# A new order of one batch's work on ScalarE, VectorE and TensorE in the attention part of an attention and mixture-of-experts kernel

## The chip, the cores and the metric

One core of one Trainium2 chip runs the whole program. The metric is the time of one execution on the device in microseconds (us); lower is better.

## What is computed

The input x holds 16 batches of 1024 rows with 256 columns. Two residual blocks follow each other, each closed by a layer norm over the columns.

```python
q = softmax(x @ Wq, axis=-1)              # over the 256 columns
k = softmax(x @ Wk, axis=-2)              # over the 1024 rows of a batch
v = x @ Wv
ctx = einsum('bnd,bne->bde', k, v) * scale
x = layernorm(x + (q @ ctx / 256) @ Wo + bo)
logits = x @ wr.T                          # 8 experts, the best two per row
# each expert takes its first 5120 rows; slot = number of the row among them
y = gelu(x[rows of e] @ w1[e] + b1[e]) @ w2[e] + b2[e]
x = layernorm(x + sum over the row's experts of gate * y)
```

## The kernel before

**Stages.** The first stage is the attention with the routing (Python block `block_a`), batch by batch. The second runs the experts (`block_b`), the third the last layer norm (`block_c`). The change touches the first alone.

**Precision.** A product in full precision is made of three products of a high and a low part (`product`, lines 681 to 687): a tensor x is split into `hi` (a rounded copy that ScalarE makes) and `lo = x - hi` (that VectorE makes). `xt_raw` is x transposed, as loaded; its parts `xt_hi`, `xt_lo` lie in the buffers that the trace calls `w_hi` and `w_lo`.

**One body per batch.** Each engine has a hand-written list of steps for batch b, called `body` (ScalarE from line 377, VectorE from 574, TensorE from 733). Engines run their lists in order and meet only by semaphores. In body b TensorE works on three batches:

- For batch b: `transpose_k(0..3)` puts the exponentials of k into the PSUM tile `t_ps`, ScalarE copies them out (`kt_out`, to `kt`), and `context(0..3)` multiplies them with `x_raw` into `g_ps` (the trace's line 761). ScalarE and VectorE split that sum into `g_hi` and `g_lo`; `maps` multiplies them with Wv·Wo into `m_ps`; VectorE scales that to `m_raw`, which is split in turn (`m_hi`, `m_lo`). `transpose_q`, `qt` on both engines and `attend(0..3)` give the output (line 685 with o_ps and g_ps), and VectorE's `residual(0..3)` adds x.
- For batch b+1: `q_next(0..3)` and `k_next(0..3)` are the logits of q and k. VectorE takes their maxima (`q_maximum` line 483, `k_maximum` line 479), ScalarE the exponentials (`q_softmax` line 355, `k_softmax` line 349). `q_next(j)` needs the PSUM tile that `q_softmax(j-1)` has read; `k_next(2)` needs the first `k_softmax`, `transpose_k(0)` of the following body the second.
- For batch b-1: VectorE computes the layer norm's `statistics`, and in `router` the two best experts (`choose`), the scores' gap times the norm's factor (`scale_gap`, line 533, which waits for GpSimd's `norm_chain`), and from TensorE's `rank` (a prefix sum over rows) the slots (`place`), the addresses (`address`) and the gates (`gates`). ScalarE takes the exponential of the gap (`gate_exp`) and applies the norm (`normalize`, two halves of four instructions). GpSimd then issues 16 scattering DMAs (`scatter`, line 320), and only after them comes its `norm_chain` for the next batch.
- For batch b+2: ScalarE makes `xt_hi` (`split_xt_hi`, line 345) and VectorE `xt_lo` (`split_xt_lo`, line 467). SyncE loads the next `xt_raw` when that is done, between the load of x and the two stores of the normalized batch.

Bodies are numbered 0 to 15. Body 0 has no work for a batch b-1, the last two have no split of x transposed, and the last one has no logits.

Of the kernel before, what the change touches and what calls it, by code (L numbers as in the profile page):

```python
# [6 lines left out]
def build(nc, x, x_t, wq, wk, wv_t, wo, wo_t, bo, bo_t, wr_t, w1, b1_t, w2, b2, out):  # L7
# [38 lines left out]
    with outer:  # L46
# [38 lines left out]
        with ExitStack() as phase:  # L85
# [254 lines left out]
            def _(act):  # L340
# [41 lines left out]
                def body(pair, u, first, last):  # L382
# [19 lines left out]

                    if more:
                        q_softmax(b + 1, 1 - u, 0, None if first else TILES * b)
                    kt_out(0)
                    kt_out(1)
                    kt_out(2)
                    if more:
                        q_softmax(b + 1, 1 - u, 1)
                    kt_out(3)  # L410
                    if split_next:
                        split_xt_hi(b + 2, u)
                    if not first:
                        gate_exp(b - 1)
                        normalize(b - 1, 1 - u, 0)
# [3 lines left out]
                    nc.scalar.activation(g_hi[:, :, :], g_sum, ACT.Copy).then_inc(g_hi_done, 1)  # L419
                    if more:  # L420
                        q_softmax(b + 1, 1 - u, 2)
# [6 lines left out]
                    if more:  # L428
                        k_softmax(b + 1, 1 - u, 0)
                        q_softmax(b + 1, 1 - u, 3)  # L430
                    if not first:
                        normalize(b - 1, 1 - u, 1)
                    qt(2)
                    qt(3)
# [13 lines left out]
            def _(dve):  # L448
# [57 lines left out]
                def router(b, u, state):  # L506
# [28 lines left out]
                    def place():  # L535
                        dve.wait_ge(rank_ready, b + 1)
                        step(V.tensor_tensor(slot[:, :, :], rank_ps, over_tiles(slot_next[:, :]), ALU.add))
                        V.tensor_tensor(slot_next[:, :], slot_next[:, :], total_ps, ALU.add)
                        step(V.tensor_tensor(late[:, :, :], slot[:, :, :], over_tiles(slot_end[:, :]), ALU.is_ge))
                        step(V.scalar_tensor_tensor(slot[:, :, :], late[:, :, :], DROPPED, slot[:, :, :], ALU.mult, ALU.add))  # L540
# [22 lines left out]
                    return choose, scale_gap, place, address, gates  # L563
# [9 lines left out]
                def body(pair, u, first, last):  # L573
# [5 lines left out]
                    if not first:  # L579
                        choose, scale_gap, place, address, gates = router(b - 1, 1 - u, {"k": 0})  # L580
# [3 lines left out]
                    if not first:  # L584
                        dve.wait_ge(r_done, TILES * b)
                        statistics(b - 1, 1 - u)
                        choose()
                    if more:
                        q_maximum(b + 1, 1 - u, 1)
                    dve.wait_ge(k_exp_done, DK * (b + 1))  # L590
# [7 lines left out]
                    if split_next:  # L598
                        split_xt_lo(b + 2, u)
# [5 lines left out]
                    dve.wait_ge(g_hi_done, b + 1)  # L605
                    V.tensor_tensor(g_lo[:, :, :], g_sum, g_hi[:, :, :].bitcast(F), ALU.subtract).then_inc(g_lo_done, 1)
# [31 lines left out]
                    residual(0)  # L638
                    qt(2)
                    residual(1)  # L640
                    qt(3)
                    if more:
                        k_maximum(b + 1, 1 - u, 1)
                    residual(2)
# [5 lines left out]
                choose, scale_gap, place, address, gates = router(NB - 1, 1, {"k": 0})  # L650
                choose()
                scale_gap()
                place()
# [28 lines left out]
            def _(pe):  # L682
# [51 lines left out]
                def body(pair, u, first, last):  # L734
# [17 lines left out]
                    def context(j):  # L752
                        if j == 0:
                            pe.wait_ge(x_loaded[u], 16 * (pair + 1))
                            if not first:
# [38 lines left out]
                    def maps():  # L794
                        pe.wait_ge(g_lo_done, b + 1)
                        if first:
                            pe.wait_ge(wvo_split, 2)
# [22 lines left out]
                    context(2)  # L820
                    if not first:
                        rank(b - 1)
                    context(3)
# [432 lines left out]
```

## Time and profile before

| | us |
|---|---|
| median of 3 runs (2379.13 to 2380.41) | 2379.3 |
| the profiled execution | 2381.19 |
| its span in the trace | 2379.4 |

The profiled execution's span is split by TensorE's work: the attention stage lasts to some 655 us, the experts to 2263 us, the last norm to the end. The view of stretches gives the busy time of each engine in a stretch and the granted clock of TensorE as a share of 2.4 GHz. The timelines list instructions by their start and duration in us; the brackets give how long the engine was idle before the instruction and who released it. A matmul's duration overlaps that of the next one, so distances are read from start to start.

### The profile page before, as it was taken

The page shows a single profiled execution, that of the slowest core. Times are in us where ns is not written, and L with a number is a line of the kernel's source. Part 1 is how long each engine was busy: PE and PEld are TensorE (multiplying, and loading weights), DVE is VectorE, ACT ScalarE, POOL GpSimd, SP SyncE. Part 2 cuts the span into 40 slices and gives each one's busy share as a digit, 9 for nine tenths or more (in the row PEclk, how much of TensorE's full clock was granted, in tenths as well). Part 3 has the DMA queues.
Part 4 walks back from the last instruction along what each step waited for, and adds up shares of the span by engine and source line. Part 5 has one row for each costly group of instructions (what it writes and reads, how often), then busy time and mean ns, then how long its engine had stood idle before and what let it go on. Part 6 is the DMA issues. An engine that isn't in the chain of part 4 may idle for free. (4 is left out here: it accounts for less than half of the span.)

```text
span 2379.4 us, 39592 instructions
## 1 busy us (share of the span) xinstructions
PE 2107.2 (89%) x13648; PEld 1903.9 (80%) x13649; DVE 1133.1 (48%) x2509; ACT 1125.1 (47%) x2009; POOL 1084.2 (46%) x1185
## 2 busy tenths in 40 slices
PE   6988888888279999999999999999999999999910
PEld 5877887787268899988989998888999888889910
DVE  3666666666443344344344334433533533333345
ACT  3454454444234444444444444444444444444437
POOL 0344645545644444444445444444444444444434
PEclk9999999999689999999999999999999999999955
DMA  5233424422234223223224232422322232323268
GB/s 190 89 124 108 124 92 127 129 77 90 71 106 86 40 49 78 46 44 80 44 44 80 44 49 41 84 42 47 78 46 44 44 44 44 44 44 48 43 204 376
DMA packets 134436, 195.29 MB, mean 82 GB/s; under 512 B 19712, under 2 KB 114816, under 8 KB 130176
## 3 DMA queue, kind: packets, MB, share of 16 engines
q0 software_dynamic: 61376, 73.19, 19.2%
q1 hardware_dynamic: 73024, 121.69, 14.9%
q8 instruction: 15, 0.25, 0.0%
q14 instruction: 21, 0.17, 0.0%
HBM read 106.67 MB, written 88.15 MB: 82 GB/s over the span
## 5 line engine op out<-in xcount | busy, mean ns | idle before, releaser
L1035 DVE TENSOR_TENSOR h_lo<-h_ps,h_hi 128x512 fp32r<-128x512 f32 x544 | 376.1, 691 | 762.8 <-ACT h_hi L1002 762.7
L997 ACT ACTIVATE h_ps<-h_ps,b_sb 128x512 f32<-128x512 f32 x544 | 360.1, 662 | 735.3 <-PE h_ps L1103 725.1
L960 POOL DMA_INDIRECT sum_rows<-y,put_idx x276 | 435.8, 1579 | 554.2 <-DVE y L1023 491.2
L1116 PE MATMUL y_ps<-w_hi,h_hi 128*128 128x256 f32 x2176 | 608.7, 280 | 12.8 <-DVE h_lo L1035 12.8
L1116 PE MATMUL y_ps<-w_hi,h_lo 128*128 128x256 f32 x2176 | 605.9, 278 | 0.0
L1116 PE MATMUL y_ps<-w_lo,h_hi 128*128 128x256 f32 x2176 | 604.9, 278 | 0.0
L1103 PE MATMUL h_ps<-bt_hi,w_hi 128*128 128x512 f32 x1088 | 434.3, 399 | 5.9 <-issue 3.5
L1116 PEld LDWEIGHTS y_ps<-w_hi,h_hi 128*128 128x128 f32 x2176 | 408.9, 188 | 36.6 <-DVE h_lo L1035 19.7
L1103 PE MATMUL h_ps<-bt_hi,w_lo 128*128 128x512 f32 x1088 | 430.3, 396 | 0.0
L1103 PE MATMUL h_ps<-bt_lo,w_hi 128*128 128x512 f32 x1088 | 429.5, 395 | 0.0
L1116 PEld LDWEIGHTS y_ps<-w_hi,h_lo 128*128 128x128 f32 x2176 | 409.2, 188 | 17.5
L1116 PEld LDWEIGHTS y_ps<-w_lo,h_hi 128*128 128x128 f32 x2176 | 409.1, 188 | 0.0
L320 POOL DMA_INDIRECT slot_table<-entry,where x256 | 254.4, 994 | 274.2 <-DVE entry L560 197.4
L1002 ACT ACTIVATE h_hi<-h_ps 128x512 fp32r<-128x512 f32 x544 | 326.0, 599 | 17.1
L949 POOL DMA_INDIRECT rows<-x_rows,pick_idx x280 | 274.2, 979 | 125.8 <-issue 64.6
L1103 PEld LDWEIGHTS h_ps<-bt_hi,w_lo 128*128 128x128 f32 x1088 | 204.9, 188 | 45.6
L1103 PEld LDWEIGHTS h_ps<-bt_hi,w_hi 128*128 128x128 f32 x1088 | 205.0, 188 | 38.0 <-issue 4.9
L1103 PEld LDWEIGHTS h_ps<-bt_lo,w_hi 128*128 128x128 f32 x1088 | 205.3, 189 | 30.5
L1051 DVE TENSOR_TENSOR y_raw<-y_ps,b_sb 128x1024 f32<-128x1024 f32 x68 | 83.2, 1224 | 144.8 <-PE y_ps L1116 144.8
L761 PE MATMUL g_ps<-kt,x_raw 128*128 128x256 f32 x512 | 123.4, 384 | 24.0 <-ACT kt L393 24.0
L355 ACT ACTIVATE q_exp<-q_ps,nq_max 128x256 f32<-128x256 f32 x128 | 59.5, 470 | 140.5 <-DVE nq_max L483 137.4
L761 PEld LDWEIGHTS g_ps<-kt,x_raw 128*128 128x128 f32 x512 | 92.4, 190 | 37.5 <-issue 17.0
(190 smaller groups left out, 2697.5 us busy)
## 6 DMA issues: line engine op xcount, KB each, us to landing
xt_raw<-in_x_t SPq DMA_DIRECT2D x16, 1024.0 KB, 4.9
x_raw<-in_x SPq DMA_DIRECT2D x16, 1024.0 KB, 7.0
w_raw<-in_w SPq DMA_DIRECT2D x16, 1024.0 KB, 7.4
x_rows<-x_sb SPq DMA_DIRECT2D x16, 1024.0 KB
sum_rows<-x_sb SPq DMA_DIRECT2D x16, 1024.0 KB
s_in<-sum_rows SPq DMA_DIRECT2D x16, 1024.0 KB, 8.8
out<-s_out SPq DMA_DIRECT2D x16, 1024.0 KB, 6.7
rows<-x_rows,pick_idx POOLq DMA_INDIRECT x280, 2.8
```

The lines of the kernel that those rows point to most:

```text
L320: pool.indirect_dma_start(out=table_dram, out_offset=bass.IndirectOffsetOnAxis(ap=where[u][:, c, t:t + 1], axis=0), in_=entry[u][:, c, t, ...
L355: nc.scalar.activation(q_exp[u][:, t, :], q_ps[:, t % 2, 0:D], ACT.Exp, bias=nq_max[:, u, t:t + 1], accum_out=zq[:, u, t:t + 1]).then_inc( ...
L761: ins = nc.tensor.matmul(g_sum[:, k, :], x_raw[u][:, t, k * P:(k + 1) * P], kt[:, j % 2, i * D:(i + 1) * D], start=(t == 0 and k == 0), st ...
L949: pool.indirect_dma_start(out=rows[u][:, t, :], out_offset=None, in_=x1_dram, in_offset=bass.IndirectOffsetOnAxis(ap=pick_idx[u][:, t:t + ...
L960: pool.indirect_dma_start(out=acc_dram, out_offset=bass.IndirectOffsetOnAxis(ap=put_idx[:, t:t + 1], axis=0), in_=y[:, t, :], in_offset=No ...
L997: nc.scalar.activation(h_ps[:, c, :], h_ps[:, c, :], ACT.Gelu_apprx_tanh, bias=b1_sb[:, bass.ds(e * FT + f, 1)]).then_inc(gelu_done, 1)
L1002: nc.scalar.activation(h_hi[:, c, :], h_ps[:, c, :], ACT.Copy).then_inc(h_hi_done, 1)
L1035: V.tensor_tensor(h_lo[:, c, :], h_ps[:, c, :], h_hi[:, c, :].bitcast(F), ALU.subtract).then_inc(h_lo_done, 1)
L1051: V.tensor_tensor(y_raw[:, :, :], y_ps[:, :, :], b2_sb[:, bass.ds(e * D, D)].rearrange("p (a d) -> p a d", a=1).broadcast_to([P, BT, D]), ...
L1103: ins = nc.tensor.matmul(h_ps[:, f % 4, :], w[:, c:c + P], v[:, k, :], start=(i == 0), stop=(i == 3 * DK - 1))
L1116: ins = nc.tensor.matmul(y_ps[:, t, :], v[:, f % 4, t * P:(t + 1) * P], w[:, c:c + D], start=(f == 0 and t % 2 == 0 and part == 0), stop=( ...
```

## The change

The same instructions run in another order.

- ScalarE: `kt_out(0)` and `kt_out(1)` come ahead of `q_softmax(0)`; `split_xt_hi` ahead of `kt_out(3)`; `q_softmax(1)` behind it. `normalize(0)` moves behind the copy to `g_hi`, `normalize(1)` behind `qt(2)` and `qt(3)`.
- VectorE: `q_maximum(1)` comes ahead of `choose`. The two steps of `place` that read the ranks from PSUM become `ranked`, directly behind `scale_gap`; then comes `g_lo`, and only then `place`, `address` and `q_maximum(2)`. `split_xt_lo` moves from behind `scale_gap` to behind `residual(0)`, late in the body. `residual(2)` comes ahead of the second `k_maximum`.
- TensorE: `rank` comes behind `context(3)`, and in body 0 the wait for the split of Wv·Wo stands at `context(0)` where it stood at `maps`.

```diff
+                    kt_out(0)
+                    kt_out(1)
                     if more:
                         q_softmax(b + 1, 1 - u, 0, None if first else TILES * b)
-                    kt_out(0)
-                    kt_out(1)
                     kt_out(2)
+                    if split_next:
+                        split_xt_hi(b + 2, u)
+                    kt_out(3)
                     if more:
                         q_softmax(b + 1, 1 - u, 1)
-                    kt_out(3)
-                    if split_next:
-                        split_xt_hi(b + 2, u)
                     if not first:
                         gate_exp(b - 1)
-                        normalize(b - 1, 1 - u, 0)
...
                     nc.scalar.activation(g_hi[:, :, :], g_sum, ACT.Copy).then_inc(g_hi_done, 1)
+                    if not first:
+                        normalize(b - 1, 1 - u, 0)
...
-                    if not first:
-                        normalize(b - 1, 1 - u, 1)
                     qt(2)
                     qt(3)
+                    if not first:
+                        normalize(b - 1, 1 - u, 1)
...
                         statistics(b - 1, 1 - u)
-                        choose()
                     if more:
                         q_maximum(b + 1, 1 - u, 1)
+                    if not first:
+                        choose()
...
                         scale_gap()
-                    if split_next:
-                        split_xt_lo(b + 2, u)
+                        ranked()
+                    dve.wait_ge(g_hi_done, b + 1)
+                    V.tensor_tensor(g_lo[:, :, :], g_sum, g_hi[:, :, :].bitcast(F), ALU.subtract).then_inc(g_lo_done, 1)
                     if not first:
                         place()
                         address(prev, scattered)
                     if more:
                         q_maximum(b + 1, 1 - u, 2)
-                    dve.wait_ge(g_hi_done, b + 1)
-                    V.tensor_tensor(g_lo[:, :, :], g_sum, g_hi[:, :, :].bitcast(F), ALU.subtract).then_inc(g_lo_done, 1)
...
                     residual(0)
+                    if split_next:
+                        split_xt_lo(b + 2, u)
                     qt(2)
                     residual(1)
                     qt(3)
+                    residual(2)
                     if more:
                         k_maximum(b + 1, 1 - u, 1)
-                    residual(2)
                     residual(3)
...
                     context(2)
+                    context(3)
                     if not first:
                         rank(b - 1)
-                    context(3)
```

## Rows read from the trace of the kernel before

**Rows 1.** The page, part 1: busy us, share of the span, instructions by engine.
```profile
PE 2107.2 (89%) x13648; PEld 1903.9 (80%) x13649; DVE 1133.1 (48%) x2509; ACT 1125.1 (47%) x2009; POOL 1084.2 (46%) x1185
```

**Rows 2.** Stretches: start:end, length, busy by engine, TensorE clock, DMA share, GB/s.
```profile
243.50:280.60 37.10, 32.84 (x219) 29.67 (x217) 24.38 (x72) 19.54 (x48) 18.55 (x21) 1.00 0.37 114
...
280.60:317.70 37.10, 32.78 (x208) 29.59 (x207) 24.49 (x72) 18.00 (x46) 18.23 (x22) 0.95 0.37 114
```

**Rows 3.** Timeline (start us, duration us): bodies' first q logits, first maximum.
```profile
38.42 0.48 PE L685 MATMUL q_ps<-wq_hi,w_hi 128*128 128x264 f32 x1
...
72.40 0.69 DVE L483 TENSOR_REDUCE nq_max<-q_ps 128x2 f32<-128x512 f32 x1 [0.98 <-PE q_ps L687]
...
252.66 0.69 DVE L483 TENSOR_REDUCE nq_max<-q_ps 128x2 f32<-128x512 f32 x1 [0.98 <-PE q_ps L687]
...
286.50 0.28 PE L685 MATMUL q_ps<-wq_hi,w_hi 128*128 128x264 f32 x1
...
288.18 0.69 DVE L483 TENSOR_REDUCE nq_max<-q_ps 128x2 f32<-128x512 f32 x1 [0.98 <-PE q_ps L687]
...
325.23 0.69 DVE L483 TENSOR_REDUCE nq_max<-q_ps 128x2 f32<-128x512 f32 x1 [0.97 <-PE q_ps L687]
...
546.25 0.69 DVE L483 TENSOR_REDUCE nq_max<-q_ps 128x2 f32<-128x512 f32 x1 [0.98 <-PE q_ps L687]
```

**Rows 4.** Timeline of TensorE around its three waits, in two neighbouring bodies.
```profile
268.02 0.39 PE L704 MATMUL k_ps<-w_hi,wk_lo 128*128 128x512 f32 x1
...
270.33 0.39 PE L685 MATMUL g_ps<-wvo_hi,g_hi 128*128 128x264 f32 x1 [1.91 <-DVE g_lo L606]
...
283.89 0.28 PE L687 MATMUL g_ps<-m_hi,qt_lo 128*128 128x264 f32 x1
...
284.94 0.39 PE L685 MATMUL o_ps<-m_hi,qt_hi 128*128 128x264 f32 x1 [0.76 <-DVE x_sb L629]
...
287.98 1.03 PE L749 MATMUL t_ps<-ident,k_exp 128*128 128x128 f32 x8
...
290.63 1.75 PE L761 MATMUL g_ps<-kt,x_raw 128*128 128x256 f32 x7 [1.62 <-ACT kt L393]
```

**Rows 5.** Timeline of TensorE at the start of the last body.
```profile
578.20 1.03 PE L749 MATMUL t_ps<-ident,k_exp 128*128 128x128 f32 x8
...
579.57 1.97 PE L761 MATMUL g_ps<-kt,x_raw 128*128 128x256 f32 x8 [0.34 <-ACT kt L393]
```

**Rows 6.** Timeline, ScalarE and VectorE in two bodies: what precedes g_lo.
```profile
300.00 2.08 ACT L365 ACTIVATE x_sb<-x_sb,nshift,rstd 128x256 f32<-128x256 f32 x4
...
300.06 2.29 DVE L467 TENSOR_TENSOR w_lo<-xt_raw,w_hi 128x2048 fp32r<-128x2048 f32 x1 [2.29 <-ACT w_hi L345]
...
305.12 0.68 DVE L606 TENSOR_TENSOR g_lo<-g_ps,g_hi 128x512 fp32r<-128x512 f32 x1
...
592.05 0.69 DVE L606 TENSOR_TENSOR g_lo<-g_ps,g_hi 128x512 fp32r<-128x512 f32 x1 [0.57 <-ACT g_hi L419]
```

**Rows 7.** Timeline of VectorE: the scaled gap (L533), the last gate (L560).
```profile
297.60 0.17 DVE L533 TENSOR_TENSOR gap<-gap,rstd 128x8 f32<-128x8 f32 x1 [0.62 <-POOL nshift L314]
...
565.04 0.17 DVE L560 TENSOR_TENSOR entry<-gap_exp,entry 128x8 f32<-128x8 f32 x1
...
589.17 0.17 DVE L533 TENSOR_TENSOR gap<-gap,rstd 128x8 f32<-128x8 f32 x1 [2.71 <-POOL nshift L314]
...
597.09 0.17 DVE L560 TENSOR_TENSOR entry<-gap_exp,entry 128x8 f32<-128x8 f32 x1
```

**Rows 8.** Timeline: a scatter DMA beside a split, and a pause.
```profile
351.11 0.98 POOL L320 DMA_INDIRECT slot_table<-entry,where  x1 [2.14 <-issue]
...
625.91 4.42 DVE L658 TENSOR_TENSOR w_lo<-w_raw,w_hi 128x4096 fp32r<-128x4096 f32 x1
...
626.86 4.43 POOL L320 DMA_INDIRECT slot_table<-entry,where  x1 [3.82 <-DVE entry L560]
```

**Rows 9.** View by tile of xt_raw, its loads' way to memory on the chip.
```profile
DMA to landing us min/median/max: 4.8/4.9/6.0
```

More of the change, by code:

```diff
@@ L430, in body @@
                         q_softmax(b + 1, 1 - u, 3)
+                    qt(2)
+                    qt(3)
                     if not first:
                         normalize(b - 1, 1 - u, 1)
-                    qt(2)
-                    qt(3)
                     if more:
@@ L533, in scale_gap, with ranked @@
                         V.tensor_tensor(gap[:, :], gap[:, :], rstd[:, :], ALU.mult).then_inc(gap_ready, 1)
-                    def place():
+                    def ranked():
                         dve.wait_ge(rank_ready, b + 1)
@@ L538, in place @@
                         V.tensor_tensor(slot_next[:, :], slot_next[:, :], total_ps, ALU.add)
+                    def place():
                         step(V.tensor_tensor(late[:, :, :], slot[:, :, :], over_tiles(slot_end[:, :]), ALU.is_ge))
@@ L561, in gates @@
                         assert state["k"] == ROUTE_STEPS, state["k"]
-                    return choose, scale_gap, place, address, gates
+                    return choose, scale_gap, ranked, place, address, gates
                 def statistics(b, u):
@@ L579, in body @@
                     if not first:
-                        choose, scale_gap, place, address, gates = router(b - 1, 1 - u, {"k": 0})
+                        choose, scale_gap, ranked, place, address, gates = router(b - 1, 1 - u, {"k": 0})
                     if more:
@@ L649, in _ @@
                 statistics(NB - 1, 1)
-                choose, scale_gap, place, address, gates = router(NB - 1, 1, {"k": 0})
+                choose, scale_gap, ranked, place, address, gates = router(NB - 1, 1, {"k": 0})
                 choose()
                 scale_gap()
+                ranked()
                 place()
@@ L754, in context @@
                             pe.wait_ge(x_loaded[u], 16 * (pair + 1))
-                            if not first:
+                            if first:
+                                pe.wait_ge(wvo_split, 2)
+                            else:
                                 pe.wait_ge(r_done, TILES * b)
@@ L795, in maps @@
                         pe.wait_ge(g_lo_done, b + 1)
-                        if first:
-                            pe.wait_ge(wvo_split, 2)
                         for o in range(DK):
```

## The prediction

> **What bounds the kernel now.** Part 1 of the page shows TensorE busy for 89% of the span and no other engine over 48% [rows 1], so I look for time in which TensorE stands still or runs slowly. The view of stretches, laid over one batch, gives 32.8 us of TensorE work in a 37.1 us body, with VectorE at 24.5, ScalarE at 18.0 and GpSimd at 18.2 us; in one neighbour the granted clock was 1.00 over the body and in the other 0.95, that is, part of it at 1.2 instead of 2.4 GHz [rows 2]. The first maximum of the q logits marks the same point of every body: from 252.66 to 288.18 are 35.52 us (no slow time), from 288.18 to 325.23 are 37.05 us [rows 3]. So one fall of the clock costs 1.53 us. The loop's other bodies repeat one of the two lengths; 8 of the 15 bodies ahead of the last have the fall. In each it comes right at `maps`, behind TensorE's wait for `g_lo`.
>
> The timeline of TensorE then shows three waits in a body [rows 4]. (a) From the first k transposes to `context(0)` pass 287.98 to 290.63 = 2.65 us; it waits for `kt`, which ScalarE copies only behind `q_softmax(0)`, which waits for VectorE's maximum. (b) From the last matmul of `k_next(0)` to `maps` pass 268.02 to 270.33 = 2.31 us, where matmuls of this kind follow each other at 0.24 us; it waits for `g_lo`. (c) In front of `attend(3)` pass 283.89 to 284.94 = 1.05 us, where 0.12 us is the pace; it waits for `residual(2)`, queued behind a `k_maximum`.
>
> **The change part by part.** Durations are those of the profiled execution, whose span is 2379.4 us inside 2381.19 us; the median is 2379.3 us. I subtract the saving from the median, as it does not depend on the 1.9 us between the two.
>
> (a) `kt_out(0)` and `(1)` ahead of `q_softmax(0)`. The last body has no `q_softmax`, so it already shows this order: 578.20 to 579.57 = 1.37 us from transposes to `context(0)` [rows 5]. Saving 2.65 - 1.37 = 1.28 us. `q_softmax(0)` gets later by two copies, some 1.1 us, and frees the tile that `q_next(1)` needs; `context(0)`, about 1.8 us long, and two transposes stand ahead of `q_next(1)` and cover that. Without them it would cost up to 1.1 us.
>
> (b) `g_lo` earlier. Now it starts at 305.12, behind the four `normalize` on ScalarE (2.08 us, ahead of `g_hi`), `split_xt_lo` (2.29 us), `place`, `address` and `q_maximum(2)` on VectorE [rows 6]. All of these move behind `g_hi` and `g_lo`. The new order needs `context(3)` for `g_hi`, the ranks for `ranked`, and the scaled gap for both. Let N be the time of the scaled gap after the body's first q logit. From N, `gate_exp`, `g_hi` and `g_lo` remain: in the last body `g_lo` began 592.05 - 589.17 = 2.9 us after the gap [rows 6, 7], of which 2.0 us were the four `normalize` that move away; 0.75 us later `maps` began. So `maps` can start at N + 1.7. TensorE gets there at 268.02 + 0.24 - 250.98 - 1.28 = 16.0 us (250.98 is 252.66 minus the 1.68 us between first logit and maximum, 286.50 to 288.18 [rows 3]). The wait is gone if N is under 14.3. That saves 2.31 - 0.24 = 2.07 us per body, and with it the 1.53 us of slow clock in 8 bodies, as no idle time as long as 1.9 us would be left. `rank` behind `context(3)` only swaps two pieces of TensorE work of 1.1 and 1.6 us.
>
> N comes from GpSimd. It issues 16 scatter DMAs after the last gate and only then the norm chain: from 565.04 + 0.17 to the next scaled gap at 589.17 pass 24.0 us [rows 7]. At 297.60 the gap waited for it too: N is 297.60 - 286.50 = 11.1 us now. In the new body the last gate falls S = 19.4 us after the start (565.21 - 544.57 = 20.6 in body 14, less 1.28 of (a)). So N = 19.4 + 24.0 - P, with P the new length of a body: 12.0 us for P = 31.4.
>
> (b') `split_xt_lo` late. It is moved past `g_lo`, and lands in VectorE's idle time ahead of `qt(2)`, some 2.8 us in the trace; ScalarE delivers `qt_hi(2)` sooner as `normalize(1)` no longer precedes it, so both arrive about together. TensorE has `k_next(2)`, `attend(1)` and `k_next(3)`, some 4.8 us, before it wants `qt_lo(2)`. No cost there; it would be up to 2.3 us if that cover went. But it now runs beside the scatter DMAs, which it never did. A row shows what that does: beside VectorE's split at 625.91 (4.42 us, until 630.33) the DMA issued at 626.86 took 4.43 us instead of 0.98 [rows 8]; it ended 0.96 us after the split. So GpSimd stood still until VectorE was through. A split of 2.29 us then costs GpSimd between nothing (if the two don't meet as they did there) and 2.3 us; I take 2.1 us, the row being of the same instruction on the same kind of operands. N becomes 14.0 us, just under the 14.3. VectorE then reaches the scaling of `m_raw` at N + 4.1 = 18.1 us instead of 17.9, and the split of `m_hi` and the later k exponential follow: 0.2 us per body.
>
> The Trainium skill ("SBUF — State Buffer", Who interferes with whom) says that a VectorE instruction with two SBUF inputs contends with a GpSimd instruction that reads SBUF, and infers that generating DMA descriptors is not held up by such a `tensor_tensor`. By that inference this term would be nought and the result 2.6 us lower; the row above speaks against it, and I go by the row.
>
> SyncE's queue: the load of `xt_raw` waits for `split_xt_lo` and is now issued some 26 us into the body instead of 16, still ahead of the two stores (`normalize(1)` ends about 3 us later) and of the load of x. It is wanted by `split_xt_hi` 10.8 us after the issue, and lands after 4.8 to 6.0 us [rows 9].
>
> (c) `residual(2)` ahead of `k_maximum`: 1.05 - 0.12 = 0.93 us saved. The second k exponential comes 0.9 us later and is wanted by the next body's transposes, behind `q_next(0)`: by my count it ends 0.1 us after TensorE is ready. So 0.1 us is given back.
>
> **The sum.** A loop body without slow clock: 35.52 - 1.28 - 2.07 - 0.93 + 0.1 + 0.2 = 31.5 us; added up piece by piece from the starts on TensorE it is 31.6, which I take. Body 0 has no router: from 38.42 to 72.40 - 1.68 it took 32.30 us, and (a), (c) and 0.1 us at `maps` leave 30.1 us. Bodies 0 to 13 took 546.25 - 1.68 - 38.42 = 506.15 us; they will take 30.1 + 13 x 31.6 = 440.9. Saved: 65.2 us. In body 14 the last gate comes 20.6 - 19.4 = 1.2 us earlier. The attention stage ends by GpSimd: last gate, 24.0 us, last body's `g_lo` and gate, 24 us more, one more scatter. In the last body gap to last gate are 8.1 us (589.17 to 597.26) [rows 7]; without the four `normalize` in front of `g_hi` 6.2. Saved: 1.9 us. GpSimd sometimes pauses 2.1 us in a scatter (the row at 351.11, seen in 2 of 16) [rows 8]. With N so close to its limit nothing hides that any more: 2 us lost. Sum: 65.2 + 1.2 + 1.9 - 2.0 = 66.3 us. Prediction 2379.3 - 66.3 = 2313.0 us. The experts and the last norm follow unchanged.
>
> **The rivals.**
> A, the forecast: the three waits close, TensorE's own work bounds the body. Bounds: 31.0 us if also the small waits close, 2305 us; 32.3 us if each costs a little more, 2322 us. Chance 0.72.
> B: the chain through GpSimd becomes the bound. Its round is S - N + 24.0 + what VectorE's split takes from it; S - N can't be under 5.5 us (the 6.2 of the last body, less what slow matmuls cost there). It decides from a loss of 2.1 us on. If split and pauses cost 4.3 us in every batch, a body takes 33.8 us: 30.1 + 13 x 33.8 = 469.5, saved 36.7 + 3.1, 2339.5 us. For it: N is within 0.3 us of its limit. Against: it needs twice the loss of the one row. Chance 0.12.
> C: TensorE still meets one wait of about 1 us in the middle of the body (ranks, or the masks that now come behind a maximum), or the clock falls in 8 bodies as before: 8 x 1.53 = 12.2 us, 2325 us. For it: the falls did not follow each wait of 1.9 us, so their condition is not plain. Against: the largest wait left is 0.4 us. Chance 0.11.
> D, the other side: the load of `xt_raw`, now 10 us later, isn't there for `split_xt_hi`. Behind that instruction on ScalarE stand `kt_out(3)`, and so `context(3)` and all TensorE work. Nothing is lost up to 12.6 us from issue to landing, beyond that every us counts in every body; the kernel gets slower than before from 17.3 us on. At 19 us a body takes 38.0 us, and the whole 2394 us. Against: the longest landing is 6.0 us [rows 9], and the stores are queued behind it, not ahead. Chance 0.05, most of it with a slower kernel.
> That the change doesn't do what it says has no room: each order is written out by hand.
>
> **How the numbers follow.** The likeliest is A with 2313.0 us. The range runs from 2302 us (below A's floor by 3 us, should GpSimd not be held at all and the tail gain more) to 2332 us, which takes in A and C (0.83) and the milder half of B's way there. A measurement tells 0.2%, 4.8 us, from no change. A, B and C are all faster: 0.95. D splits into 0.01 within 0.2% and 0.04 slower.
>
> **What the profile after would show.** The first q maxima 31.6 us apart; `context(0)` 1.37 us behind the transposes; no wait in front of `maps` and `attend(3)`; a granted clock of 1.00 through the bodies; one scatter DMA in each batch with some 3 us instead of 0.98; the scaled gap at 14 us after the first logit. The forecast is wrong if `maps` still waits for `g_lo` (then B: the gap later than 14.3 us), if `split_xt_hi` waits for a DMA (D), or if the clock still falls (C).

## The result and the profile after

| | before | after |
|---|---|---|
| median, us | 2379.86 (2379.13 to 2381.72, 4 runs) | 2311.22 (2310.56 to 2312.31, 4 runs) |
| span of the profiled execution, us | 2379.4 | 2308.9 |
| ratio to before, with its 95% interval | | 0.9711 (0.9694 to 0.9728) |

The change saves 68.6 us; the forecast was 66.3 us, and 2313.0 us stands 1.8 us above the median. In a later session the changed kernel took 2311.62 us beside 2378.98 us of the kernel before, the ratio 0.9718 (0.9702 to 0.9734).

The page's part 1 of the kernel after, and the view of stretches over one body; they answer [rows 1] and [rows 2].

```profile
PE 2091.7 (91%) x13648; PEld 1895.9 (82%) x13649; DVE 1133.4 (49%) x2509; ACT 1123.8 (49%) x2009; POOL 1109.3 (48%) x1185
```

```profile
256.70:288.16 31.46, 30.94 (x207) 28.27 (x206) 24.54 (x73) 17.87 (x44) 20.09 (x20) 1.00 0.43 134
```

The body is 31.46 us long, TensorE has 30.94 us of work in it, and the clock is 1.00. TensorE's whole work is 15.5 us less than before, with as many instructions; by my estimate 12.2 us of that is time that the slow clock had added (eight falls of 1.53 us). GpSimd's is 25.1 us more, with as many instructions too; experiment 5 shows where.

The timeline of the kernel after, one fence each for the whole loop, for TensorE in one body, and for the other engines in that body. Columns as in [rows 3].

```profile
38.06 0.48 PE L691 MATMUL q_ps<-wq_hi,w_hi 128*128 128x264 f32 x1
...
258.38 0.69 DVE L484 TENSOR_REDUCE nq_max<-q_ps 128x2 f32<-128x512 f32 x1 [0.65 <-PE q_ps L693]
...
289.85 0.69 DVE L484 TENSOR_REDUCE nq_max<-q_ps 128x2 f32<-128x512 f32 x1 [0.66 <-PE q_ps L693]
...
478.17 0.29 PE L691 MATMUL q_ps<-wq_hi,w_hi 128*128 128x264 f32 x1
```

```profile
258.23 1.09 PE L755 MATMUL t_ps<-ident,k_exp 128*128 128x128 f32 x8
...
259.66 1.97 PE L769 MATMUL g_ps<-kt,x_raw 128*128 128x256 f32 x8 [0.34 <-ACT kt L393]
...
272.64 0.39 PE L710 MATMUL k_ps<-w_hi,wk_lo 128*128 128x512 f32 x1
272.87 0.28 PE L691 MATMUL g_ps<-wvo_hi,g_hi 128*128 128x264 f32 x1
...
280.31 0.50 PE L710 MATMUL k_ps<-w_hi,wk_hi 128*128 128x512 f32 x1 [0.18 <-ACT k_exp L349]
```

```profile
262.59 1.91 ACT L345 ACTIVATE w_hi<-xt_raw 128x2048 fp32r<-128x2048 f32 x1
...
270.73 0.17 DVE L534 TENSOR_TENSOR gap<-gap,rstd 128x8 f32<-128x8 f32 x1 [2.12 <-POOL nshift L314]
...
271.66 0.69 DVE L604 TENSOR_TENSOR g_lo<-g_ps,g_hi 128x512 fp32r<-128x512 f32 x1 [0.43 <-ACT g_hi L418]
...
276.03 0.17 DVE L563 TENSOR_TENSOR entry<-gap_exp,entry 128x8 f32<-128x8 f32 x1
...
280.93 2.28 DVE L468 TENSOR_TENSOR w_lo<-xt_raw,w_hi 128x2048 fp32r<-128x2048 f32 x1
...
281.10 2.95 POOL L320 DMA_INDIRECT slot_table<-entry,where  x1 [0.31 <-issue]
```

From 258.38 to 289.85 are 31.47 us, where [rows 3] had 35.52 or 37.05. `context(0)` starts 1.43 us behind the transposes (2.65 before) and `maps` 0.23 us behind the last k matmul (2.31 before). No wait in front of `attend(3)` is left in this body. The only new one is 0.18 us for the first k exponential, ahead of `k_next(2)`. The scaled gap stands at 270.73 - 256.70 = 14.03 us (256.70 is the body's first q logit, 1.68 us ahead of the maximum at 258.38). `split_xt_hi` at 262.59 has no wait in brackets: `xt_raw` was there. And the scatter DMA beside `split_xt_lo` took 2.95 us instead of 0.97.

What TensorE waited for, in the view of waits (us in total, times, longest), of the kernel before and then of the kernel after:

```profile
PE g_ps L685 <- DVE g_lo L606: 28.3, 14, 3.9
PE g_ps L761 <- ACT kt L393: 24.0, 16, 1.6
PE o_ps L685 <- DVE x_sb L629: 11.5, 16, 0.8
```

```profile
PE g_ps L769 <- ACT kt L393: 4.9, 16, 0.3
PE g_ps L691 <- DVE g_lo L604: 2.5, 2, 1.8
PE k_ps L710 <- ACT k_exp L349: 1.9, 10, 0.2
PE o_ps L691 <- DVE x_sb L632: 0.3, 1, 0.3
```

The three waits fall by 25.8, 19.1 and 11.2 us. Two come up: 1.9 us for the first k exponential, in ten bodies, and 1.3 us ahead of the last body's transposes, for the second k exponential. That leaves 52.9 us. Eight falls of the clock at 1.53 us [rows 2, 3] add 12.2 us. Together 65.1 of the 70.5 us between the two spans. Most of the other 5.4 us is, by my estimate, that the view counts less than what is lost from start to start: 1.91 us at `maps` where the distance is 2.31 - 0.24 = 2.07, and 0.76 us at `attend(3)` where it is 0.93.

**What sets the length of a body now.** Follow the round through GpSimd in the rows above. From the scaled gap at 270.73 to the end of the last gate at 276.20 are 5.47 us. VectorE works through them with one wait, 0.43 us ahead of `g_lo` for ScalarE's `g_hi`. From that gate GpSimd's scatter and norm chain lead to the next scaled gap:

```profile
302.19 0.17 DVE L534 TENSOR_TENSOR gap<-gap,rstd 128x8 f32<-128x8 f32 x1 [2.12 <-POOL nshift L314]
```

That is 302.19 - 276.20 = 25.99 us, and 5.47 + 25.99 = 31.46 us, one body. Any two gaps are a body apart; what tells is that no link of this round waits for anything outside it. ScalarE's `g_hi` comes behind the exponential that waits for the gap, `m_raw` follows the q maximum without a wait, and the gap waits 2.12 us for GpSimd. So the round sets the body, and TensorE's 0.18 us in front of `k_next(2)` is where it feels that. Experiment 4 and a pause of GpSimd ("The margin", below) bear it out. TensorE's own work isn't far below: with the round shortened in experiment 4 the bodies are 31.35 us long.

### The profile page after: what moved, and what is told of

Its sections match the earlier page's. It is cut to its first block and busy times, and to the rows that moved or that the text cites. A ratio compares the mean times of both kernels' runs of the same rounds, so it can differ in the third digit from the quotient of the medians.

```text
span 2308.9 us, 39587 instructions
## 1 busy us (share of the span) xinstructions
PE 2091.7 (91%) x13648; PEld 1895.9 (82%) x13649; DVE 1133.4 (49%) x2509; ACT 1123.8 (49%) x2009; POOL 1109.3 (48%) x1185
## 5 line engine op out<-in xcount | busy, mean ns | idle before, releaser
L1122 PE MATMUL y_ps<-w_hi,h_hi 128*128 128x256 f32 x2176 | 608.9, 280 | 12.8 <-DVE h_lo L1041 12.8
L320 POOL DMA_INDIRECT slot_table<-entry,where x256 | 280.3, 1095 | 181.4 <-DVE entry L563 104.7
L952 POOL COPY pick_idx<-table 128x4 int32 (+1 forms) x70 | 13.1, 187 | 183.7 <-DMA sum_rows<-y,put_idx 153.4
```

What stands on the lines that cost most here:

```text
L320: pool.indirect_dma_start(out=table_dram, out_offset=bass.IndirectOffsetOnAxis(ap=where[u][:, c, t:t + 1], axis=0), in_=entry[u][:, c, t, ...
L952: G.tensor_copy(pick_idx[u][:, :], table[:, bass.ds(n * BT + BT, BT), 0]).then_inc(idx_ready[u], 1)
L1122: ins = nc.tensor.matmul(y_ps[:, t, :], v[:, f % 4, t * P:(t + 1) * P], w[:, c:c + D], start=(f == 0 and t % 2 == 0 and part == 0), stop=( ...
```

## Experiments

**Two kinds of session.** The experiments ran in five sessions. In one the kernel before took 2379 us and the kernels beside it can be compared in microseconds. In the four others, called disturbed here, it took 2578 to 2595 us: in every kernel traced there, TensorE, VectorE and ScalarE stand still for several us in each body from the third on. (The kernel before has no trace from such a session.) There only ratios are compared, and rows of the first two bodies, which are undisturbed. The view of stretches shows it, of the kernel of experiment 7 in a disturbed session and then of the changed kernel:

```profile
60.00:91.00 31.00, 30.32 (x202) 27.65 (x201) 23.88 (x71) 15.85 (x40) 3.81 (x6) 1.00 0.21 68
91.00:122.00 31.00, 24.83 (x133) 21.71 (x132) 17.62 (x52) 12.90 (x31) 18.67 (x19) 0.83 0.44 137
```

```profile
60.00:91.00 31.00, 30.66 (x205) 27.97 (x204) 24.15 (x72) 15.98 (x41) 4.48 (x6) 1.00 0.20 68
91.00:122.00 31.00, 30.75 (x205) 27.96 (x204) 24.08 (x72) 17.61 (x45) 19.80 (x21) 1.00 0.44 137
```

Up to 91 us the two are nearly alike. In the next 31 us the first one gets 133 matmuls done instead of 205, at a clock of 0.83, with the same DMA share of 0.44. In its timeline TensorE is idle for 5.23 us up to 108.52 (`context(0)`), ScalarE for 7.94 us up to 107.86 and VectorE for 3.57 us up to 105.03, while GpSimd goes on with a scatter DMA each 1.28 us.

**1. The changed kernel again**, unaltered, in the undisturbed session. It is the base for experiments 2 to 4.

> The changed kernel itself, unaltered, beside the kernels that follow on one chip. On the chips of the earlier experiments the kernel before took 2579 to 2595 us because all engines pause together in the attention stage from body 2 on. Theory 1 (the pauses are a property of the chip and add to each kernel what its bodies meet): where the kernel before takes some 2380 us this one takes 2311 us, bodies 31.5 us apart; where it takes some 2580 us this one takes 2430 to 2450 us, a ratio of 0.945 to 0.95, since it meets fewer pauses in shorter bodies. Rival (the pauses take a fixed time whatever the order): the difference stays 69 us, a ratio of 0.973.

Measured 2311.62 us (2309.90 to 2312.98) beside 2378.98, the ratio 0.9718. The session had no such pauses, so this run can't say how the changed kernel stands to before in a disturbed one; that stays open. What it gives is a base: bodies of 31.5 us (257.67 to 289.16 between first maxima), and one of 32.75. Its profiled execution took 2309.90 us, the shortest of the four.

**2. Part (a) undone: `kt_out` behind `q_softmax(0)`.**

```diff
-                    kt_out(0)
-                    kt_out(1)
                     if more:
                         q_softmax(b + 1, 1 - u, 0, None if first else TILES * b)
+                    kt_out(0)
+                    kt_out(1)
```

It ran in a disturbed session first.

> The changed kernel with one part undone: kt_out(0) and kt_out(1) stand behind q_softmax(0) again. Theory (three waits that add up): context(0) starts 2.65 us behind the k transposes instead of 1.37, every body gets 1.2 to 1.28 us longer, 14 bodies, 17 us: 2328 us. Rival (the round through GpSimd sets the length of a body and hides this): that round is 31.5 us whatever TensorE waits for ahead of context(0), unless the last gate gets later too; with it hidden the time stays within 3 us of 2311.

Measured 2444.20 us beside 2578.60, the ratio 0.9475 (0.9459 to 0.9491). The size of (a) can't be taken from it. Its second body, undisturbed, has a wait of 1.56 us at `context(0)` and is 32.47 us long between first q logits, where the changed kernel has 0.34 and 31.24 us. Then the undisturbed session:

> The changed kernel with kt_out(0) and kt_out(1) behind q_softmax(0) again. Theory (a): each body is longer by what context(0) waits more, 1.22 us (1.56 instead of 0.34, as body 1 of the first run showed: 32.47 instead of 31.24 us), so 15 to 19 us more than the changed kernel on the same chip, 2326 to 2330 us on a chip where that takes 2311. Rival (context(0) only borrows the time from a wait that comes later in the body): under 5 us more.

Measured 2324.40 us (2323.36 to 2325.27), 12.8 us more than the changed kernel. The timeline of TensorE:

```profile
266.83 1.09 PE L755 MATMUL t_ps<-ident,k_exp 128*128 128x128 f32 x8
...
269.44 1.75 PE L769 MATMUL g_ps<-kt,x_raw 128*128 128x256 f32 x7 [1.52 <-ACT kt L393]
```

The wait is back as expected, and a body costs a little less than expected: 32.5 us, 1.0 us more and not 1.22. TensorE alone had 31.35 us to the round's 31.46, so the first 0.1 us is hidden, and TensorE's waits of 0.2 us on the first k exponential are gone from all bodies but one. GpSimd's round now has 1 us of slack: the gap waits 1.1 to 1.2 us for it in most bodies instead of 2.1, and the body that a GpSimd pause lengthens to 32.75 us in the base is 32.80 here, 0.3 us more than its neighbours.

How much it is in all depends on which executions are compared. By the medians it is 12.8 us. The two profiled executions, 2325.27 and 2309.90 us, are the longest of the one kernel and the shortest of the other and lie 15.4 us apart; between these two, the experts' first gathering DMA comes 15.3 us later (604.16, there 588.87). So (a) is worth 13 to 15 us on top of the rest, at or just under the lower end of the theory's 15 to 19 us; the rival's 5 us is out. The same order alone, in the kernel before, was not measured.

**3. Part (b) undone on ScalarE: `normalize(0)` ahead of `g_hi`.**

```diff
                         gate_exp(b - 1)
+                        normalize(b - 1, 1 - u, 0)
                     act.wait_ge(kt_used, PAIRS * (b + 1))
...
                     nc.scalar.activation(g_hi[:, :, :], g_sum, ACT.Copy).then_inc(g_hi_done, 1)
-                    if not first:
-                        normalize(b - 1, 1 - u, 0)
```

> The changed kernel with one part undone: normalize(0) stands ahead of the copy to g_hi again. Theory: the scaled gap comes 14.0 us into the body, and the four normalize (2.0 us) then stand between it and g_hi, so g_lo is ready at 17.7 us where TensorE wants it at 16.0; the wait at maps comes back with 1.7 to 2.0 us per body, 26 us, and with it the clock's falls in up to half of the bodies, 9 us: 2337 to 2348 us. Rival (the wait at maps came from split_xt_lo alone, which is still late here): within 5 us of 2311, clock 1.00.

In the disturbed session 2458.26 us beside 2578.60, 0.9539 (0.9519 to 0.9558), and its second body is 31.24 us as in the changed kernel: no scatter has delayed the scaled gap there yet. Size again from the undisturbed session:

> The changed kernel with normalize(0) ahead of the copy to g_hi again. Theory (b): g_hi follows the scaled gap at 14.0 us by 2.08 us more, maps at 17.8 instead of 15.7 us after the first logit, and TensorE gets there at 16.0: 1.8 us more in each of 13 bodies (23 us), and the clock falls again in some of them, up to 8 falls of 1.5 us: 23 to 36 us more than the changed kernel on the same chip. Rival (the normalize is hidden, VectorE's order alone brought the gain): under 5 us more, and no wait at maps.

Measured 2338.47 us (2337.35 to 2338.77), 26.9 us more than the changed kernel. The timeline, all engines:

```profile
248.39 0.17 DVE L533 TENSOR_TENSOR gap<-gap,rstd 128x8 f32<-128x8 f32 x1 [2.13 <-POOL nshift L314]
...
248.71 2.06 ACT L365 ACTIVATE x_sb<-x_sb,nshift,rstd 128x256 f32<-128x256 f32 x4
...
250.67 0.57 ACT L419 ACTIVATE g_hi<-g_ps 128x512 fp32r<-128x512 f32 x1
...
252.03 0.39 PE L690 MATMUL g_ps<-wvo_hi,g_hi 128*128 128x264 f32 x1 [1.36 <-DVE g_lo L603]
```

The chain stands there link by link: gap, four `normalize`, `g_hi`, `g_lo`, `maps`, 3.64 us from first to last, against 2.14 us from gap to `maps` in the kernel after. The rival is out: the wait at `maps` is back, and the time is inside the theory's 23 to 36 us. But its sum was another one. `maps` starts 17.70 us into the body instead of 16.17, 1.53 us later, and yet the bodies are 33.45 us long, 2.0 us more. The four `normalize` stand in the round through GpSimd too, as the gates come behind `g_lo` in VectorE's list:

```profile
255.63 0.17 DVE L562 TENSOR_TENSOR entry<-gap_exp,entry 128x8 f32<-128x8 f32 x1
...
281.84 0.17 DVE L533 TENSOR_TENSOR gap<-gap,rstd 128x8 f32<-128x8 f32 x1 [2.13 <-POOL nshift L314]
```

From gap to last gate are 255.80 - 248.39 = 7.41 us instead of 5.47, from there to the next gap 26.04, together 33.45 us. So it is the longer round that costs 2.0 us a body; the theory had looked at `maps` alone. The other part of the theory fell, too: the clock. Eleven waits of 1.30 to 1.38 us at this place were followed by none of its falls; the only one in the loop came behind a wait of 2.58 us. Stretches of that kernel, behind a short wait and behind the long one:

```profile
252.00:255.50 3.50, 3.47 (x23) 3.16 (x24) 3.16 (x14) 0.98 (x6) 0.00 (x0) 1.00 0.00 0
...
353.50:357.00 3.50, 3.41 (x16) 3.13 (x17) 3.17 (x15) 0.91 (x4) 0.00 (x0) 0.67 0.00 0
```

In the kernel before, the eight falls came behind waits of 1.86 to 2.12 us at the same place, and two waits of 1.91 and 1.86 us had none [rows 2, 4]. So a wait of 1.9 us may or may not cost the clock. Nor is one of 1.3 us always free: in the last body of experiment 4 the clock is at half behind waits of 1.31 and 0.34 us. TensorE's timeline and the stretch:

```profile
509.43 1.09 PE L760 MATMUL t_ps<-ident,k_exp 128*128 128x128 f32 x8 [1.31 <-ACT k_exp L354]
...
512.00:513.00 1.00, 1.00 (x4) 0.82 (x3) 0.93 (x11) 0.00 (x0) 0.27 (x1) 0.50 0.99 308
```

**4. GpSimd's chain inside the scatter**, a version that goes further than the change: `norm_chain` comes behind six of the eight row tiles of the scatter instead of behind all. A tile has two DMAs, so it stands behind the twelfth of 16, and the other four follow it. (The second of the two expectations below says "behind the sixth", which is the tile.)

```diff
                     if not first:
                         norm_chain(b - 1)
-                        scatter(b - 1, 1 - u)
+                        if not (isinstance(pair, int) and b == 1):
+                            scatter(b - 2, u, range(HEAD, TILES))
+                        scatter(b - 1, 1 - u, range(HEAD))
...
+                HEAD = 6
```

It ran in both kinds of session.

> The changed kernel with GpSimd's norm chain for batch b-1 put ahead of the last 4 of the 16 scatter DMAs of batch b-2, where its input has just come in; nothing else. Theory: the scaled gap no longer waits for the whole scatter, it comes at 11.7 us into the body instead of 14.0, so VectorE's chain to the last gate has 2 us of slack and a body falls from 31.46 to TensorE's own 31.2; 13 bodies, 3 us. In the last body the gap waits 3.5 us now: 3 us won. At the end the norm chain of batch 15 needn't wait for all of scatter 14 and the last scatter follows it at once: 5 us. Sum 11 us less than the changed kernel, 2300 us where the kernel before takes 2379. Rival (TensorE alone bounds the bodies): the same without the first term, 8 us, 2303 us.

Disturbed: 2422.84 us beside 2590.01, 0.9350 (0.9330 to 0.9369), the lowest ratio of all.

> The changed kernel with GpSimd's norm chain moved into the 16 scatter DMAs, behind the sixth, so that the scaled gap of a body no longer waits for all 16. Theory (in the changed kernel only the tail still waits for GpSimd, N = 14.0 us being just under the 14.3 us limit): the bodies keep 31.5 us, the one body lengthened by a GpSimd pause (32.7 us) goes back to 31.5, and the tail, where the last scaled gap stood 7.35 us behind GpSimd, gains 3 to 6 us: 4 to 8 us less than the changed kernel on the same chip; more where the chip's pauses delay GpSimd past its limit in every body. Rival (GpSimd's own sum of work sets the end): no difference.

Undisturbed: 2305.78 us (2302.73 to 2307.09) beside 2311.62, 5.8 us less, ratio to before 0.9689 (0.9673 to 0.9705). It is the fastest kernel of this study. The timeline of VectorE, a scaled gap in the loop:

```profile
268.90 0.16 DVE L539 TENSOR_TENSOR gap<-gap,rstd 128x8 f32<-128x8 f32 x1
```

It waits for nothing any more (2.12 us in the kernel after), and the body still takes 31.35 us, 0.1 us less than the round of the kernel after. That is TensorE's own work, and its waits for the first k exponential are gone. So GpSimd's round did bound the body, but only by that 0.1 us. No body is lengthened by a pause, though GpSimd still has one of 2.28 us at 311.98. The last gap comes 6.1 us earlier than in the changed kernel beside it (546.54, there 552.65), and the experts' first gather 4.8 us earlier (584.11, there 588.87). Of the 4.8 us the bodies give 1.2 (fourth q maximum of body 14 at 499.27, there 500.45), the tail the rest.

**5. What holds GpSimd.** The split is replaced, from the third batch on, by an instruction of VectorE that reads the same `xt_raw` for the same 2.28 us, but has one input; the low part of x transposed stays that of an earlier batch, so the sums of this kernel leave it out.

```diff
                     dve.wait_ge(xt_hi_done, b + 1)
-                    V.tensor_tensor(xt_lo[u], xt_raw[:, :], xt_hi[u].bitcast(F), ALU.subtract).then_inc(xt_lo_done, 1)
+                    V.reduce_max(row_max[:, :], xt_raw[:, :], X).then_inc(xt_lo_done, 1)
```

> The changed kernel, its split_xt_lo from batch 2 on replaced by a maximum over xt_raw: the same place, as many columns, but one input in SBUF instead of two; the low halves of x transposed are left out. Theory (VectorE instructions with two SBUF inputs hold GpSimd's DMA instructions): the scatter DMA beside it takes 0.97 us instead of 2.95, the scaled gap comes at 12 us, the body falls by 0.2 us, 2 to 3 us in all. Rival (any long VectorE instruction holds them): 2.95 us stays and so does the time.

The timeline of the second body, VectorE and GpSimd, then part 5 of the page (busy us, mean ns, idle before) for the scatter DMAs of the kernels before, after and this one:

```profile
91.84 0.97 POOL L321 DMA_INDIRECT slot_table<-entry,where  x1 [0.30 <-issue]
...
92.81 2.28 DVE L472 TENSOR_REDUCE row_max<-xt_raw 128x1 f32<-128x2048 f32 x1
...
93.11 0.97 POOL L321 DMA_INDIRECT slot_table<-entry,where  x1 [0.30 <-issue]
```

```profile
L320 POOL DMA_INDIRECT slot_table<-entry,where x256 | 254.4, 994 | 274.2 <-DVE entry L560 197.4
```

```profile
L320 POOL DMA_INDIRECT slot_table<-entry,where x256 | 280.3, 1095 | 181.4 <-DVE entry L563 104.7
```

```profile
L321 POOL DMA_INDIRECT slot_table<-entry,where x256 | 254.0, 992 | 249.7 <-DVE entry L567 172.9
```

Two scatter DMAs start beside the reduction, at 93.11 and 94.39, and take 0.97 us each. Over the kernel the change adds 25.9 us to the 256 DMAs (280.3 against 254.4), some 2.0 us in each of 13 bodies, and with one input all of it is gone (254.0). So it isn't the length of the VectorE instruction that holds the DMA. Two things are gone with the subtraction: its second input from SBUF, and its 2048 columns of output to SBUF. The kernel before tells them apart. Its `qt_lo` subtracts an SBUF tile from a PSUM tile and writes 512 columns to SBUF:

```profile
239.12 0.69 DVE L619 TENSOR_TENSOR qt_lo<-t_ps,qt_hi 128x512 fp32r<-128x512 f32 x1 [1.28 <-ACT qt_hi L401]
...
239.20 0.97 POOL L320 DMA_INDIRECT slot_table<-entry,where  x1 [0.31 <-issue]
```

Sixteen scatter DMAs of that kernel start while a `qt_lo` still has 0.1 to 0.66 us to go, and each takes 0.97 or 0.98 us; so writing to SBUF with one input from there does not hold them. `m_lo`, which has two SBUF inputs, runs 0.22 us into a DMA in the kernel after, and that one takes 1.18 us. Order matters too: a DMA that had started 0.03 to 0.96 us ahead of a split took 0.97 or 0.98 us, and one that starts during a split ends some 0.85 us after it. The time, 2533.69 beside 2594.92 us, 0.9763 (0.9742 to 0.9784), is that of a disturbed session without the changed kernel beside it, and I draw nothing from it.

**6. The split alone moved late**, in the kernel before.

```diff
                         scale_gap()
-                    if split_next:
-                        split_xt_lo(b + 2, u)
...
                     residual(0)
+                    if split_next:
+                        split_xt_lo(b + 2, u)
```

> The kernel before with one part of the change alone: split_xt_lo late, behind residual(0). Theory: this by itself takes 2.2 us from VectorE's queue ahead of g_lo, so that maps stops waiting: 2.0 us in each of 13 bodies and the 8 falls of the clock (12 us) are saved, 38 us, 2341 us; the load of xt_raw is no trouble, one scatter DMA in each batch takes some 3 us. Rival 1 (ScalarE's four normalize ahead of g_hi hold g_lo anyway): under 10 us saved. Rival 2 (the late load of xt_raw or the held scatter DMA costs what is won): no gain.

Measured 2473.59 us beside 2578.60, 0.9591 (0.9575 to 0.9607), in a disturbed session. In its second body the wait at `maps` is gone, which is 1.61 us in that body of the kernel before, and a DMA is held for 2.81 us. So in a body where GpSimd isn't late yet the split was what `g_lo` stood behind; rival 1, ScalarE's `normalize`, is out there. In the bodies that follow it isn't tested.

**7. `k_maximum` ahead of `residual(2)` again (part (c) undone).**

```diff
-                    residual(2)
                     if more:
                         k_maximum(b + 1, 1 - u, 1)
+                    residual(2)
                     residual(3)
```

> The changed kernel with one part undone: the second k_maximum stands ahead of residual(2) again. Theory: attend(3) waits again, 0.8 to 0.93 us per body, 14 bodies: 11 to 13 us more, 2323 us. Rival (the second k exponential, which then comes 0.9 us sooner, gives as much back): within 2 us of 2311.

> The changed kernel with the second k_maximum ahead of residual(2) again, on a chip like that of the last four runs (before 2379 us, the changed kernel 2312 us) if one is had. Theory (c) as predicted: attend(3) waits 0.76 us again and each of 15 bodies is 0.8 us longer, 12.5 us in all. Rival (the 0.76 us of the kernel before held a part that came from the late g_lo and goes with it, as the second body of the first run hints: wait 0.34 us, body 31.56 instead of 31.24 us): 0.3 us a body, 4 to 5 us in all.

Both runs fell into disturbed sessions: 2450.95 beside 2578.60, 0.9498 (0.9481 to 0.9516), and 2456.41 beside 2577.84, 0.9543 (0.9502 to 0.9584). Left are the first bodies. TensorE's timeline at `attend(3)` of the second body, of this kernel and then of the kernel before:

```profile
99.23 0.36 PE L691 MATMUL o_ps<-m_hi,qt_hi 128*128 128x264 f32 x1 [0.34 <-DVE x_sb L632]
```

```profile
104.43 0.36 PE L685 MATMUL o_ps<-m_hi,qt_hi 128*128 128x264 f32 x1 [0.83 <-DVE x_sb L629]
```

The wait is 0.34 us and the body 31.56 us in the first run and 31.60 in the second, instead of 31.24. The kernel before waits 0.83 us there. So in this body (c) alone is worth 0.3 us, as in the rival, and other parts of the change had taken the other 0.5 us. The reason that the rival gives, the late `g_lo`, doesn't hold: in experiment 6 `maps` waits no more in this body and `attend(3)` waits 0.81 us. In the steady bodies the size of (c) alone is not measured.

**8. GpSimd with 0.95 us more work ahead of the scatter**, to push the scaled gap past the limit of 14.3 us.

```diff
                     wait_apart(pool, slots_ready, b + 1)
+                    nc.gpsimd.memset(idle[:, :], 0.0)
                     for t in range(TILES):
```

> The changed kernel with one more instruction on GpSimd ahead of each batch's scatter, filling a buffer of 128x1024, some 1 us. Theory (the round through GpSimd and TensorE's own work are level, 31.5 us): every us on GpSimd now counts, a body gets 0.7 to 1.0 us longer, 13 bodies, and 2 us at the end: 11 to 15 us more. Rival (TensorE alone bounds the body, GpSimd has slack): only the end gets longer, 2 to 3 us more.

2483.65 beside 2594.92 us, 0.9570 (0.9553 to 0.9587), disturbed: inconclusive on the limit. The added instruction took 0.95 us, and the DMA beside the split 2.51 us in the second body. What speaks on the limit is the round above and a pause that occurs by itself, below.

## Why the prediction was right, step by step

**Which waits bind.** Right for the kernel before. The falls of the three waits and of the clock make up 65.1 of the 70.5 us, and undoing (a) or one half of (b) brings each wait back at its place.

**What bounds the body after.** Not as forecast, though the number holds. Rival A had TensorE's own work as the bound, at 31.6 us; it is 31.35. Rival B had the round through GpSimd, S - N + 24.0 and the loss to the split, deciding from a loss of 2.1 us on. S - N is 5.47, the loss 2.0, the round 31.46 us: B's formula gives the body. The two lie 0.1 us apart, and so the time came out right whichever won. That is in part luck.

**(a)** Put at 1.28 us a body. The wait fell by 1.22 us ([rows 4] against 1.43 us from transposes to `context(0)`). Undone alone it costs 1.0 us a body and 13 to 15 us in all.

**(b)** Put at 2.07 us a body and the clock's 12.2 us. Undoing one half of it, the four `normalize`, cost 26.9 us, 2.0 us a body. The later `maps` accounts for 1.53 of them, the longer round through GpSimd for all. The working `N + 1.7` and `16.0` holds: gap at 14.03, `maps` 2.14 us later without a wait, since TensorE gets there at 272.87 - 256.70 = 16.17 us. The clock no longer falls in the loop, as forecast.

**(b')** Put at 2.1 us of GpSimd time a body, between 0 and 2.3; it was 2.0. N was forecast at 14.0 and is 14.03. The row of the DMA beside a split carried the right conclusion [rows 8], and experiment 5 shows which instructions do it. The inference of the Trainium skill ("SBUF — State Buffer", Who interferes with whom), that generating descriptors is not held by a `tensor_tensor`, does not agree with 2.95 instead of 0.97 us in this trace. These DMAs take their addresses from `where` in SBUF; whether one without such a read is held, no run here shows.

**The load of `xt_raw`** was issued at 283.37, ahead of both stores (286.71 and 287.40) and the load of x (289.37), as described, and no `split_xt_hi` waited in the loop. Rival D did not occur.

**(c)** Put at 0.93 us with 0.1 given back. The waits for `x_sb` fell by 11.2 us over 15 bodies, 0.75 a body. But experiment 7 has only 0.3 us of that from (c) itself, in the one body that it can tell of; the rest came with the other parts. The 0.1 us given back isn't there in the loop: TensorE's 0.18 us at `k_next(2)` is for the first k exponential, which (c) doesn't move. The later second one shows once, 1.3 us ahead of the last body's transposes.

**The margin.** I took N under 14.3 us as the limit and put two GpSimd pauses at 2 us lost. For `maps` the limit was near: it starts 1.68 us behind the gap when it has to wait, and TensorE is there at 16.17, so 14.5 us. But behind the gap stands all of VectorE's list to `m_raw`, `m_lo` and the k maximum, and there nothing was to spare. One pause came in the loop. GpSimd idled 2.05 us instead of 0.30, the DMA beside the split then took 2.46 instead of 2.95 us, and so the next gap came 1.26 us late:

```profile
311.75 0.98 POOL L320 DMA_INDIRECT slot_table<-entry,where  x1 [2.05 <-issue]
313.03 2.46 POOL L320 DMA_INDIRECT slot_table<-entry,where  x1 [0.30 <-issue]
...
334.92 0.17 DVE L534 TENSOR_TENSOR gap<-gap,rstd 128x8 f32<-128x8 f32 x1 [3.40 <-POOL nshift L314]
...
336.60 0.39 PE L691 MATMUL g_ps<-wvo_hi,g_hi 128*128 128x264 f32 x1 [0.67 <-DVE g_lo L604]
```

N is 15.31 us in that body, `maps` starts at 16.99 instead of 16.17, and the body is 32.73 instead of 31.46 us long: the 1.27 us came through whole. GpSimd had nothing to spare.

**The sum.** Bodies 0 to 13 were put at 440.9 us; 38.06 to 478.17 are 440.1. The last gate of body 14 was put at 19.4 us; it ends at 497.57, 19.4 us in. From gap to last gate in the last body I had 6.2 us; it is 527.71 - 521.58 = 6.1. The timeline of VectorE:

```profile
497.40 0.17 DVE L563 TENSOR_TENSOR entry<-gap_exp,entry 128x8 f32<-128x8 f32 x1
...
521.58 0.17 DVE L534 TENSOR_TENSOR gap<-gap,rstd 128x8 f32<-128x8 f32 x1 [3.47 <-POOL nshift L314]
...
527.54 0.17 DVE L563 TENSOR_TENSOR entry<-gap_exp,entry 128x8 f32<-128x8 f32 x1
...
553.49 0.17 DVE L534 TENSOR_TENSOR gap<-gap,rstd 128x8 f32<-128x8 f32 x1 [7.35 <-POOL nshift L314]
```

With the 2.0 us for pauses the bodies were put at 442.9 us, so they came out 2.8 us shorter. Body 0 took 30.35 instead of 30.1 us, the other 13 took 31.4 on average without the pause instead of 31.6, and the pause cost 1.3 instead of 2.0 us. By the medians the forecast is 2.3 us too small; the two profiled executions lie 70.5 us apart. In the tail time still lies: the last gap waits 7.35 us for GpSimd, and experiment 4 took back some 3.6 us there.

## What to carry to other kernels

Where one engine is 90% busy, list its waits in one body with what each waits for, follow each back to the step that is queued in front of it for no reason, and check in the last loop iteration, where some of that work is missing, what the shorter chain costs. Then add up every closed round, here from scaled gap to last gate, through the scatter and back to the gap, and compare it with the busiest engine's own work: a wait that is gone can leave a round that is as long. Here 31.46 us stood against 31.35, and a delay of GpSimd that had been free now came through whole. Put long VectorE instructions with two inputs where GpSimd issues no DMAs, or count their length into GpSimd's time.

## What the runs showed of the hardware

- A scatter DMA of GpSimd that takes 0.97 us took 2.95 us when it started during a VectorE subtraction of 2.28 us with two SBUF inputs. It took 0.97 us beside a VectorE reduction of 2.28 us with one, beside subtractions of 0.69 us with one input from PSUM, and when it had started ahead of the subtraction.
- TensorE's clock did not fall behind eleven waits of 1.30 to 1.38 us at `maps` nor behind those of 1.34 to 1.53 us at `context(0)`. It fell behind one of 2.58 us (0.67 over the next 3.5 us), behind 8 of the 10 of 1.86 to 2.12 us in the kernel before, and in one last body behind 1.31 and 0.34 us. So the length of the wait alone doesn't tell.
- GpSimd idles 2.0 to 2.3 us instead of 0.30 between two scatter DMAs, twice in each undisturbed trace (at 311.75 and 531.80 in the kernel after). No row shows why.
- In four of five sessions all kernels took some 5 to 9% longer, the kernel before 2578 to 2595 instead of 2379 us, with pauses of TensorE, VectorE and ScalarE in each body from the third on, as in the stretch at 91 us above. One chip had sessions of both kinds. What causes it is open. The ratio to the kernel before was lower in these sessions for each of the three kernels that ran in both (0.935 against 0.969 in experiment 4, 0.948 against 0.977 in experiment 2, 0.954 against 0.983 in experiment 3). Their order is the same in both; the sizes don't carry over.
